# A state-space layer: half of the states' inputs on ScalarE, the convolved rows and delta times u on GpSimd, delta one state later

## The reference

```python
proj = xn @ W_in + b_in
u, res = jnp.split(proj, 2, axis=-1)
up = jnp.pad(u, ((0, 0), (k - 1, 0), (0, 0)))
u = sum((up[:, i:i + seq, :] * conv_w[i] for i in range(k))) + conv_b
u = jax.nn.silu(u)
x_dbl = u @ W_x
dt, Bm, Cm = jnp.split(x_dbl, [DT_RANK, DT_RANK + N_STATE], axis=-1)
delta = jax.nn.softplus(dt @ W_dt + b_dt)
A = -jnp.exp(A_log)
# scan over the tokens, for each channel and state:
#   h = exp(delta * A) * h + (delta * u) * B;   y = sum over states of h * C
y = _selective_scan(u, delta, A, Bm, Cm, D)      # ... + u * D
y = y * jax.nn.silu(res)
return y @ W_out + b_out + x
```

## Time and profile before

| | us |
|---|---|
| median of 3 runs | 2640.59 (2640.28 to 2643.39) |
| profiled execution, its own time | 2641.36 |
| span of the profiled execution | 2639.6 |
| state-space layer within it | about 1716 to 2304 |

### The profile page before, as it was taken

How to read it: one execution, slowest core, us unless ns; L and a number is a source line. 1 busy time by engine, 2 the same in 40 slices (tenths; PEclk the granted TensorE clock), 3 DMA queues, 4 the chain that set the end, 5 groups by cost and what they waited for, 6 DMA issues and landing times. The chain is left out here.

```text
span 2639.6 us, 49063 instructions
## 1 busy us (share of the span) xinstructions
PE 2032.7 (77%) x16544; PEld 1509.7 (57%) x16544; DVE 1710.9 (65%) x4178; ACT 1390.5 (53%) x2993; POOL 1209.5 (46%) x1233
## 2 busy tenths in 40 slices
PE   5999999999986783196599996858888888732870
PEld 3666666666775673175255555746677776531560
DVE  5777777777667573012677773759999999846113
ACT  4665656575432373032265554658888888520223
POOL 5655545464310005454321213557777777501662
PEclk8999999999996595598599997979999999955885
DMA  8300000000020000122333340000000000010113
GB/s 240 84 2 2 1 2 2 2 1 2 2 72 0 0 0 32 57 67 78 96 82 86 85 131 1 0 1 1 0 0 0 0 0 0 0 32 8 46 43 97
DMA packets 104254, 89.49 MB, mean 34 GB/s; under 512 B 12076, under 2 KB 91206, under 8 KB 104006
## 3 DMA queue, kind: packets, MB, share of 16 engines
q1 hardware_dynamic: 96934, 72.67, 10.2%
q0 software_dynamic: 7168, 14.73, 1.8%
HBM read 59.02 MB, written 40.96 MB: 38 GB/s over the span
## 5 line engine op out<-in xcount | busy, mean ns | idle before, releaser
L3342 POOL TENSOR_SCALAR mb_w<-mb_duT,mb_bT 128x256 f32<-128x256 f32 x384 | 354.8, 944 | 110.5 <-ACT mb_duT L3220 99.3
L3278 DVE TENSOR_TENSOR_SCAN mb_hs<-mb_dA,bank 128x512 f32<-128x512 f32 x256 | 302.2, 1206 | 16.7 <-PE bank L3377 10.1
L38 POOL TENSOR_TENSOR scrap<-ones 128x1 f32<-128x1 f32 x64 | 12.5, 195 | 470.1 <-DVE gla_ss L414 262.7
L3328 ACT ACTIVATE mb_dA<-mb_delta,mb_A 128x255 f32<-128x255 f32 x512 | 216.5, 496 | 0.2
L2083 ACT ACTIVATE e_hid<-bank,e_b 128x512 f32<-128x512 f32 (+1 forms) x128 | 79.3, 634 | 256.3 <-PE bank L2127 188.5
L3377 PE MATMUL bank<-ident,mb_w 128*128 128x128 f32 x1024 | 160.7, 287 | 65.4 <-DVE mb_hs L3278 56.3
L2501 DVE TENSOR_REDUCE ra_mx<-bank 128x2 f32<-128x512 f32 x256 | 163.7, 685 | 61.6 <-PE bank L2355 59.1
L2591 ACT ACTIVATE ra_pT<-bank 128x512 f32<-128x512 f32 x256 | 141.2, 600 | 114.5 <-PE bank L2377 114.2
L3377 PEld LDWEIGHTS bank<-ident,mb_w 128*128 128x128 f32 x1024 | 119.6, 148 | 96.2 <-DVE mb_hs L3278 68.7
L3399 PE MATMUL bank<-ident,mb_hc 128*128 128x128 f32 x1024 | 143.4, 285 | 31.7 <-DVE mb_hc L3288 31.4
L565 DVE TENSOR_TENSOR gla_mid<-bank,gla_ex 128x512 f32<-128x512 f32 x128 | 88.3, 690 | 122.5 <-ACT gla_ex L551 122.4
(11 more groups left out here) (541 smaller groups left out, 5784.7 us busy)
## 6 DMA issues: line engine op xcount, KB each, us to landing
results<-const_empty SPq DMA_DIRECT2D x2, 4096.0 KB
e_got<-results SPq DMA_DIRECT2D x32, 256.0 KB, 3.4
rope_rows<-ra_part SPq DMA_DIRECT2D x48, 128.0 KB, 1.9
ra_k<-rope_rows SPq DMA_DIRECT2D x32, 192.0 KB
ra_q<-rope_rows SPq DMA_DIRECT2D x32, 192.0 KB
queue<-const_spare_rows SPq DMA_DIRECT2D x1, 4128.0 KB
e_x<-queue SPq DMA_DIRECT2D x8, 516.0 KB
e_w<-in_L_ffn_w SPq DMA_DIRECT2D x2, 2048.0 KB, 8.2
```

The source lines that it names most:

```text
L3278: dve.tensor_tensor_scan(hs[n // 2 % 2][:, n % 2, :, :].rearrange("p c t -> p (c t)"), dA[n % RD][:, :, :].rearrange("p c t -> p (c t)"), ...
L3328: ins = act.activation(dA[n % RD][:, c, 1:SEQ], delta[k][:, c, 1:SEQ], ACT.Exp, scale=A[:, c, n:n + 1])
L3342: ins = pool.tensor_scalar(w[n % RH][:, h, :], duT[k][:, h, :], bT[k][:, h, n:n + 1], None, ALU.mult)
```

## The change

- `by_act` (L3331) names every odd state, so ACT makes 8 of the 16 inputs of a sequence, and POOL 8 instead of 12. `act_start` makes w(1) and w(3).
- The convolved rows uc move from DVE to POOL, as two passes, e1 x cv and then + cv (`pool_convolved`), at POOL's n = 8 (after w(8)).
- delta times u moves from DVE to POOL (`pool_scaled`), at POOL's n = 14 (after w(14)).
- delta (DVE's stage 6) goes from n = 10 to n = 11; PE's stage 6 (the transposes of delta times u) from 11 to 12; ACT's stage 8 (duT) from 11 to 12, so stage 9 now comes before it.
- For the first sequence POOL does both new steps between its two powers for the norm (`pool_rs`, `pool_rs2`).

```diff
     def dve_prepare(dve, s, k, stage):
         if stage == 4:
-            dve.wait_ge(rc_ready, s + 1)
-            dve.scalar_tensor_tensor(out=uc[k][:, :, :], in0=e1[:, :, :], scalar=1.0, in1=cv[:, :, :],
-                                     op0=ALU.add, op1=ALU.mult).then_inc(uc_ready, 1)
+            return
...
-            dve.wait_ge(dl_ready, s + 1)
-            dve.tensor_tensor(z[:, :, :], delta[k][:, :, :], uc[k][:, :, :], ALU.mult).then_inc(du_ready, 1)
...
     def by_act(n):
-        return n % RH == RH - 1
-
-    PER_POOL, PER_ACT = NS - NS // RH, NS // RH
+        return n % 2 == 1
+
+    PER_ENGINE = NS // 2
...
+    def pool_convolved(pool, s, k):
+
+        pool.wait_ge(rc_ready, s + 1)
+        if s >= 2:
+            pool.wait_ge(yy_ready, s - 1)
+        pool.tensor_tensor(uc[k][:, :, :], e1[:, :, :], cv[:, :, :], ALU.mult).then_inc(up_ready, 1)
+        pool.wait_ge(up_ready, s + 1)
+        pool.tensor_tensor(uc[k][:, :, :], uc[k][:, :, :], cv[:, :, :], ALU.add).then_inc(uc_ready, 1)
+
+    def pool_scaled(pool, s, k):
+
+        pool.wait_ge(dl_ready, s + 1)
+        pool.tensor_tensor(z[:, :, :], delta[k][:, :, :], uc[k][:, :, :], ALU.mult).then_inc(du_ready, 1)
+
...
         if by_act(n):
-            pe.wait_ge(wa_ready, s * PER_ACT + (n // RH + 1))
+            pe.wait_ge(wa_ready, s * PER_ENGINE + (n // 2 + 1))
         else:
-            pe.wait_ge(w_ready, s * PER_POOL + (n - n // RH + 1))
+            pe.wait_ge(w_ready, s * PER_ENGINE + (n // 2 + 1))
...
-    DVE_WHEN = {6: (4,), 8: (5,), 9: (7,), 10: (6,)}
-    ACT_WHEN = {1: (0,), 3: (1, 2), 7: (4,), 8: (5,), 9: (6,), 11: (8, 9)}
-    PE_WHEN = {0: (0,), 1: (1,), 2: (2,), 6: (4,), 7: (5,), 8: (7,), 10: (9,), 11: (6,)}
-    IN_PLACE, BACK, FINISH, POOL_GATE, POOL_FINISH, OUT, RESIDUAL = 0, 2, 4, 4, 7, 7, 9
+    DVE_WHEN = {6: (4,), 8: (5,), 9: (7,), 11: (6,)}
+    ACT_WHEN = {1: (0,), 3: (1, 2), 7: (4,), 8: (5,), 9: (6,), 11: (9,), 12: (8,)}
+    PE_WHEN = {0: (0,), 1: (1,), 2: (2,), 6: (4,), 7: (5,), 8: (7,), 10: (9,), 12: (6,)}
+    IN_PLACE, BACK, FINISH, POOL_GATE, POOL_FINISH, POOL_CONVOLVED, POOL_SCALED, OUT, RESIDUAL =\
+        0, 2, 4, 4, 7, 8, 14, 7, 9
...
-        act_inputs(act, 0, 0, RH - 1)
+        act_inputs(act, 0, 0, 1)
+        act_inputs(act, 0, 0, 3)
...
             pool_rs(pool, 1)
+            pool_convolved(pool, 0, 0)
+            pool_scaled(pool, 0, 0)
             pool_rs2(pool, 1)
...
+                    if n == POOL_CONVOLVED and s + 1 < NSEQ:
+                        pool_convolved(pool, s + 1, 1 - s % 2)
+                    if n == POOL_SCALED and s + 1 < NSEQ:
+                        pool_scaled(pool, s + 1, 1 - s % 2)
```

More of the change, by code:

```diff
@@ L3094, in mamba @@
              "ez", "lz", "dl", "du", "duTp", "duT", "dA", "w", "dbu", "cp", "hs", "hc", "y", "yy", "op", "x0", "x",
-             "st", "mv", "mvs", "yT", "yb", "wa", "yg", "gp"]
+             "st", "mv", "mvs", "yT", "yb", "wa", "yg", "gp", "up"]
     (xn_ready, xT_psum, xT_ready, ur_psum, ub_ready, rc_ready, r_psum, r_ready, er_ready,
@@ L3099, in mamba @@
      dA_ready, w_ready, dbu_psum, bc_psum, hs_ready, hc_ready, y_psum, yy_ready, o_psum, x0_ready, x_ready,
-     st_ready, mv_ready, mvs_ready, yT_ready, yb_psum, wa_ready, yg_ready, gp_ready) = [sig(n) for n in names]
+     st_ready, mv_ready, mvs_ready, yT_ready, yb_psum, wa_ready, yg_ready, gp_ready, up_ready) = [sig(n) for n in names]
     DB, RC, YB = g.pb[0:2], g.pb[2:4], g.pb[4]
```

## The result

The changed kernel takes 2677.2 us in the median (2674.1 to 2686.2), the kernel before 2641.4 (2640.3 to 2643.4). The ratio is 1.0137, 95% interval 1.0121 to 1.0153: slower by 1.4%. The forecast was 2677 with a range of 2660 to 2694. The profiled execution took 2678.0 us, with a span of 2676.2.

A forecast was written before the change was run, and what follows sets the result against it. It took ACT's unbroken work from `z` to `xT`, then PE's leg back to `z`, as the bound. Legs 30.8, start 1.8, end 0.4 and clock 3.5 made 36.5 us, giving 2677 us, range 2660 to 2694.

The forecast's parts named there:

- The loop that sets the pace: State-space layer: ACT without a stop from `z` to `xT` (18.27 us, +2.2 forecast), then PE from `xT` to `z` (16.13).
- The sum: Whole kernel: 30.8 for 14 legs, 1.8 start, 0.4 end, 3.5 clock; 36.5 us added.
- The start: Ahead of the first scan: POOL's uc and product, with some given back by w(1) from ACT; +1.8 us at first `xT`.
- The 1.9 for uc on POOL: First sequence, ahead of the first scan: uc takes 2.56 us on POOL in place of 0.68, +1.9.
- The end: Last sequence: prepares nothing, but its scan 0 comes 14.7 instead of 14.3 us after `z`; +0.4 us.
- ACT's four pairs: New input pairs at ACT's n = 1, 5, 9, 13: n = 5 swallowed by waiting, three cost 2.4 us, 0.2 met by waits.
- Taken from DVE, worth 0: DVE loses uc (0.68 us) and delta times u (0.69); their 1.37 us a sequence gain 0.
- Delta and duT later, hidden with 1.0 us of cover: DVE stalls 1.5 us before next scan 0, yet `result` could come at 18.2 against ACT's 19.2 us after `z`.
- The wait for delta: Sign on DVE: about 1 us before delta, about 1.5 before next scan 0, over 2 before scan 4.
- POOL: POOL busy 22.5 us a sequence; uc ready before PE's `W_dx`, cost 0 with 0.4 us of cover.
- The granted clock: PE's slow stretches after longer waits, lengthening inputs and sums before `result`: 0.25 us a sequence, 3.5 in all.
- rival D: PE's slow stretch hits convolution or sums in most sequences, 1.2 to 1.7 us each; 2687 to 2697, chance 0.13.

The follow-up runs named there:

- e3_pair_behind_xT: Changed kernel with ACT's pair for w(5), at n = 1, moved behind the copy to `xT`; 2668.0 us, ratio 1.0099.
- the two doses: Kernel before plus one idle activation pair on ACT: at n = 9 between `z` and `xT` 2652.9 us, at n = 5 in a wait 2642.0 us.
- v3_start_on_dve: v1_pairs_in_waits with the first sequence's convolved rows and product back on DVE; 2609.1 us, ratio 0.9874.
- e4_delta_as_before: Changed kernel with the three order tables (delta, its transposes, duT) as in the kernel before; 2687.7 us, ratio 1.0180.
- e1_inputs_only: Kernel before with only by_act changed, so ACT makes eight states' inputs; 2686.6 us, ratio 1.0171.
- e2_moves_only: Changed kernel with by_act undone (12 of 16 inputs on POOL), all moves kept; 2676.7 us, ratio 1.0132.
- e7_pool_moves_only: Kernel before with only the two moves to POOL (uc, delta times u), inputs and tables as before; 2651.3 us, ratio 1.0033.
- v2_residual_later: v1_pairs_in_waits with ACT's in-place residual at n = 2, behind `xT`, instead of n = 0; 2612.2 us, ratio 0.9910.
- v1_pairs_in_waits: Changed kernel with ACT making only w(5), w(7), w(9), w(11), outside `z` to `xT`, and duT ahead of the gate; 2610.8 us, ratio 0.9890.

## Why the prediction was right, and where not

**The loop that sets the pace** was right. The leg from `z` to `xT` was forecast to grow by 2.2 and grew by 2.19; the other stayed (16.13 to 16.11). e3_pair_behind_xT shows that it is the place of the pairs and not their number, and the two doses show the same in the kernel before.

**The sum** came out at 36.5 against 36.6 in the span, but not in each term. The 14 turns took 515.2 us against 481.7, 33.4 more (forecast 34.3: 30.8 and 3.5). If all had been of the usual 36.53, they would have taken 511.4; the 3.8 above that is the clock's, forecast 3.5. The start was mis-sized: from the stage's first `xT` to the second it is 33.75 us against 30.41, so 3.3 more, not 1.8; v3_start_on_dve takes off 3.65 there. The 1.9 for uc on POOL came out, but PE's two groups of matmuls behind it, `W_dx` and `W_dt`, run at the lower clock, which the forecast counted in the 14 turns only. `W_dx` in the kernel before and in the changed one:

```profile
1735.99 1.13 PE L3251 MATMUL bank<-mb_uc,mb_W_dx 128*128 128x256 f32 x4 [2.32 <-DVE mb_uc L3143]
```

```profile
1734.44 2.03 PE L3247 MATMUL bank<-mb_uc,mb_W_dx 128*128 128x256 f32 x4 [4.27 <-POOL mb_uc L3356]
```

The end (last `xT` to the last scan, 59.5 against 57.8) cost 1.6, not 0.4: its scan 0 came 15.3 us after `z`, not 14.7, at the lower clock; the other 0.6 was not traced. Together 38.4 in the stage. The execution was 2.9 us quicker ahead of the stage, where nothing was changed, and 1.1 slower behind it. That the sum came within 0.1 us is luck: start and end together cost 2.7 more than forecast, which was cancelled by 0.9 less in the turns and by this 1.8 outside the stage.

**ACT's four pairs**: right. The one at n = 5 was swallowed, and with it went the wait for `mid`; the wait before `z` grew instead to 1.49.

**Taken from DVE, worth 0**: right. e4_delta_as_before has the two moves to POOL that e1_inputs_only lacks, and is otherwise the same: 525.7 us for the 14 turns against 526.9, 2687.7 against 2686.6 in all. What the changed kernel gets back against both, 9 to 10 us, comes with the later tables. For that the prediction had no term.

**Delta and duT later, hidden with 1.0 us of cover**: in the usual turn of the changed kernel it was. Scan 0 was forecast 14.7 us after `z`; it came at 15.5, 0.5 of it from the clock. The wait for delta was 1.15 against 1.0, that before scan 0 2.31 against 1.5, that before scan 4 1.68 against "over 2". The cover was worked out for the chain through scan 0; e2_moves_only shows a second one behind duT, through POOL's w(1) and w(2), which makes `result` wait 0.9 us when POOL makes all three inputs. The changed kernel avoids it because w(1) is ACT's.

**POOL**: uc made PE wait only in the first sequence, and POOL was busy 22.1 us (22.5). The risk was elsewhere than I put it: not uc but the w(9) behind it, where POOL makes that one (0.7 us a turn in e7_pool_moves_only).

**The granted clock**: the size in the turns was right, the place half. I expected it in the sums before `result`; it was there (0.23) and as much in the transposes before duT (0.31). The kernel before had shown this second place, 0.50 and 0.83 us ahead of duT in two turns, and the prediction read only the turn with 0.05. That a slow stretch on the convolution costs 1.6 to 1.7 us a turn, rival D, is shown by e4_delta_as_before. (D's upper end was added up wrong: 20 us on the forecast without its 3.5 is 2694, not 2697.) In the changed kernel it doesn't occur, and with the earlier tables it does, so the tables, which the prediction had only as a cost, are what keeps it away.

What stays open: which idle times of PE make the clock fall. In the kernel before PE's wait of 2.43 us stands in each of 13 steady turns, and the granted clock is 1.00 in six of them and 0.95 in seven. Nor was it tried how far the other leg (16.1 us) can be shortened.

## What to carry to other kernels

Find the leg in which an engine has no wait and ask of each moved instruction whether it lands in that leg; the busiest engine need not be the one that sets the pace, and an engine with 6 us to spare may have none of it where it is needed. A step that is hidden is hidden behind a certain other one: before taking the cover away or judging the step alone, compute the next chain's arrival, and through every engine that makes something for it: here it was POOL's third input, not the first. When two chains arrive within 0.2 us of each other, shortening one alone gains little (0.1 us for 0.77 in v2_residual_later).

## What the hardware showed that was not expected

In e4_delta_as_before a wait of 2.39 us on PE stands ahead of a matmul group that then takes 3.68 us in place of 2.00. The wait alone doesn't make it so: in e1_inputs_only the same 2.39 stands in four turns ahead of a convolution at full clock, and a slow stretch falls on the transposes ahead of duT instead. The exchange of three tables, without any change of work, was worth some 10 us in the whole kernel. In v1_pairs_in_waits, where the longest wait of PE in the turn shown is 1.5 us, the granted clock is 1.00 from 1780 to 2220 us, in the kernel before 0.98.

An activation pair of 2 x 240 columns with bf16 output held ACT for 0.58 us, the pair of 2 x 256 with f32 output for 0.80. The two differ in their scale operand too (a constant against a tile's column), and no run tells which of these it is.
